# Three changes of instruction order in a fused sequence-mix and BitNet feed-forward kernel: statistics tiles moved into the rounding loop, weight preparation redistributed over the pairs, and the stages of the output projection re-sequenced

## What is computed

```python
# state-space mix with 256 complex states, then LayerNorm
Bu_re, Bu_im = x @ gB_re.T, x @ gB_im.T
h[t] = A * h[t-1] + Bu[t]                      # complex
y = H_re @ C_re.T - H_im @ C_im.T + D * x
x1 = layernorm(x + y)
# feed-forward with 8-bit activations and ternary weights
h = x1 * rsqrt(mean(x1**2) + eps) * norm_w
q(a) = clip(round(a * s), -127, 127) / s       # s = 127 / max|a| of the token
w(W) = clip(round(W / m), -1, 1) * m           # m = mean|W| of the whole matrix
value, gate = split(q(h) @ w(w_gv).T)          # 16384 outputs
h2 = value * silu(gate)                        # 8192 wide
out = layernorm(x1 + (x1 + q(h2) @ w(w_out).T))
```

## Time and profile before

| | |
|---|---|
| time, median of 3 runs (lowest, highest) | 6579.42 us (6553.91, 6587.52) |
| the profiled execution: its own time | 6587.52 us |
| its span on the slowest core (core 1) | 6585.9 us |
| spans of the 8 cores | 6539.1 to 6585.9 us |
| mean granted TensorE clock | 0.776 to 0.780 on all cores |
| TensorE matmul busy | 3338.1 us (51%) |
| VectorE (DVE) | 2360.6 us (36%) |
| ScalarE (ACT) | 1403.7 us (21%) |
| GpSimd (POOL) | 859.6 us (13%) |

### The profile page before, as it was taken

One profiled execution on the slowest core, in us unless ns is written; L12 is line 12 of the kernel. 1 busy time (PEld: TensorE's weight loads), 2 busy tenths in 40 slices (PEclk: granted clock), 3 DMA queues, 4 the chain that ended last, 5 costly groups with the idle time before them and its releaser, 6 DMA issues.

```text
span 6585.9 us, 44872 instructions; the slowest of 8 cores (6539.1 to 6585.9 us)
## 1 busy us (share of the span) xinstructions
PE 3338.1 (51%) x13489; PEld 1315.9 (20%) x13489; DVE 2360.6 (36%) x3177; ACT 1403.7 (21%) x1134; POOL 859.6 (13%) x933
## 2 busy tenths in 40 slices
PE   1223303319998897566556880604560455055545
PEld 0100000004333333222222330201120122012211
DVE  1323464562332232222222336174227422732242
ACT  2222122124444443344444320000000000000000
POOL 0110010011111111111111111010201020102002
PEclk9756656659999998788878995857785788578877
DMA  8234364365555553444544511303430343034334
GB/s 223 91 114 124 100 204 132 91 175 155 145 151 138 143 150 105 134 147 139 151 144 138 135 44 35 102 29 94 136 99 29 96 140 95 29 98 140 92 90 128
DMA packets 682744, 774.87 MB, mean 118 GB/s; under 512 B 24412, under 2 KB 585727, under 8 KB 649223
## 3 DMA queue, kind: packets, MB, share of 16 engines
q1 hardware_dynamic: 617768, 444.78, 25.3%
q10 hardware_dynamic: 27648, 201.34, 9.5%
q0 software_dynamic: 37088, 125.87, 5.7%
HBM read 662.83 MB, written 117.44 MB: 118 GB/s over the span
## 4 chain that ended last, share of the span: by engine, by line
DMA 25%; PE 24%; DVE 22%; issue 12%; ACT 8%; POOL 7%; DVEq 1%; SPq 0%; ACTq 0%; POOLq 0%
PE psA L971 7%; DMA WR<-wq2sp 6%; PE psA L776 5%; DMA P<-wgvT 4%; PE psB L776 3%; ACT HBF L728 3%; POOL CBF L796 3%; DMA x1sp<-OTS 3%; DMA WR<-wgvT 2%; DMA WOF<-woutT 2%; PE psB L971 2%; DMA WOF<-wgvT 2%; DMA WR<-woutT 2%; DMA wq2sp<-P 2%; DVE HBF L788 2%
## 5 line engine op out<-in xcount | busy, mean ns | idle before, releaser
L971 PE MATMUL psA<-P,WR 128*128 128x512 bf16 x3072 | 700.7, 385 | 899.2 <-DMA WR<-wq2sp 892.2
L776 PE MATMUL psA<-P,MNA 128*128 128x512 bf16 x2048 | 498.4, 403 | 276.4 <-DVE CBF L801 266.9
L776 PE MATMUL psA<-P,CBF 128*128 128x512 bf16 x2048 | 492.7, 399 | 261.3 <-DVE CBF L801 245.7
L971 PEld LDWEIGHTS psA<-P,WR 128*128 128x128 bf16 x3072 | 294.9, 99 | 1320.6 <-issue 1002.9
L776 PE MATMUL psB<-P,CBF 128*128 128x512 bf16 x2048 | 457.4, 379 | 9.6
L776 PE MATMUL psB<-P,MNA 128*128 128x512 bf16 x2048 | 457.4, 379 | 9.6
L796 POOL TENSOR_TENSOR CBF<-HBF,P 128x1024 f32<-128x1024 f32 x128 | 299.2, 2337 | 1222.1 <-ACT HBF L793 1186.2
L1028 ACT ACTIVATE P<-Z2S 128x512 f32<-128x512 f32 x64 | 40.3, 629 | 1654.2 <-DVE Z2S L1008 1654.2
L776 PEld LDWEIGHTS psA<-P,MNA 128*128 128x128 bf16 x2048 | 205.5, 102 | 568.4 <-issue 368.4
L776 PEld LDWEIGHTS psA<-P,CBF 128*128 128x128 bf16 x2048 | 204.4, 102 | 548.7 <-issue 345.4
L793 ACT ACTIVATE HBF<-HBF 128x1024 f32<-128x1024 f32 x128 | 135.2, 1057 | 716.7 <-DVE HBF L788 716.7
(11 more groups left out here) (213 smaller groups left out, 3951.8 us busy)
## 6 DMA issues: line engine op xcount, KB each, us to landing
P<-wgvT SPq DMA_DIRECT2D x128, 1024.0 KB
WR<-wq2sp SPq DMA_DIRECT2D x256, 512.0 KB
WOF<-wgvT ACTq DMA_DIRECT2D x64, 1024.0 KB, 5.8
WR<-wgvT ACTq DMA_DIRECT2D x64, 1024.0 KB, 5.8
WOF<-woutT SPq DMA_DIRECT2D x64, 1024.0 KB
h2sp<-CBF POOLq DMA_DIRECT2D x128, 256.0 KB, 4.6
WOF<-woutT ACTq DMA_DIRECT2D x32, 1024.0 KB, 6.5
WR<-woutT ACTq DMA_DIRECT2D x32, 1024.0 KB, 5.8
```

What stands on the lines that cost most here:

```text
L776: sv=sv, last=last: t.matmul(PS[:, (vg * 2 + tq) * 512:(vg * 2 + tq + 1) * 512], WQap(sv + vg)[:, a * 128:(a + 1) * 128], P1[:, a * T + th ...
L971: seg=seg, PSm=PSm: t.matmul(PSm(ds), WR[:, sl * 2048 + jj * 256 + ds * 128: sl * 2048 + jj * 256 + (ds + 1) * 128], P1[:, seg * 16384 + j ...
```

## The change

Three edits.

1. The mix of a tile becomes a function `emit_mix_a(q, a)`. The 16 tiles of quarter 0 are written ahead of the loop. Tile a of quarter q+1 is written inside the round loop of quarter q, behind the rounding of tile a. Rows, normalize, token maxima and the 20 chunks of |w_gv| stay where they were.
2. In the pairs, four chunks of |w_out| are written per pair for p < 16 (two for p < 32 before); the scale of w_out follows at p = 16 (p = 32); then two preparations per pair (three).
3. In the output projection, segment 0 of the next quarter is multiplied before the rows and the output of the present one.

```diff
     emit_xload(0)
+    for a in range(DT):
+        emit_mix_a(0, a)
     for q in range(NQ):
-        for a in range(DT):
...
         b.op("vector", lambda v: v.tensor_scalar(
             repr_(0), psB[0:1, 1024:1536], 1.0 / D, None, OP.mult),
...
             round_neg(k, P1[:, a * T + q * 512:a * T + (q + 1) * 512],
                       R("P1", a * T + q * 512, a * T + (q + 1) * 512, es=2))
+            if q + 1 < NQ:
+                emit_mix_a(q + 1, a)
         for ci in range(50 + q * 20, min(NGV, 70 + q * 20)):
             emit_abs_chunk(wgv_chunk(ci), ci)
...
-        if p < 32:
-            emit_abs_chunk(wout_chunk(2 * p), NGV + 2 * p)
-            emit_abs_chunk(wout_chunk(2 * p + 1), NGV + 2 * p + 1)
-        elif p == 32:
+        if p < 16:
+            for ii in range(4):
+                emit_abs_chunk(wout_chunk(4 * p + ii), NGV + 4 * p + ii)
+        elif p == 16:
...
         elif woj[0] < PAIRS:
-            n = 3 if p < 60 else 8
-            for _ in range(n):
+            for _ in range(2):
...
     d_rowsQ(0)
     d_quant(0, 0)
+    d_mm(0, 0)
+    d_quant(0, 1)
     for q in range(NQ):
-        d_mm(q, 0)
-        d_quant(q, 1)
         if q + 1 < NQ:
             d_rowsQ(q + 1)
             d_quant(q + 1, 0)
         d_mm(q, 1)
+        if q + 1 < NQ:
+            d_quant(q + 1, 1)
+            d_mm(q + 1, 0)
         d_rowsL(q)
         d_apply(q)
```

More of the change, by code:

```diff
@@ L527, in emit_xload @@
                 writes=R("P2", lo * 512, (lo + 4) * 512))
+    def emit_mix_a(q, a):
+        bank = a % 2
+        for im in range(2):
+            for nh in range(2):
+                CT = CBF if nh == 0 else CBF2
+                cn = "CBF" if nh == 0 else "CBF2"
+                HT = HBF if im == 0 else HBF2
+                hn = "HBF" if im == 0 else "HBF2"
+                b.op("tensor", lambda t, q=q, a=a, im=im, nh=nh, bank=bank,
+                     CT=CT, HT=HT: t.matmul(
+                    PSA(bank), CT[:, im * D + a * 128:im * D + (a + 1) * 128],
+                    HT[:, nh * T + q * 512:nh * T + (q + 1) * 512],
+                    start=(im == 0 and nh == 0), stop=(im == 1 and nh == 1)),
+                    reads=R(cn, im * D + a * 128, im * D + (a + 1) * 128, es=2) +
+                          R(hn, nh * T + q * 512, nh * T + (q + 1) * 512, es=2),
+                    writes=[RA(bank)], inc=(im == 1 and nh == 1))
+        b.op("vector", lambda v, a=a, bank=bank: v.scalar_tensor_tensor(
+            P2[:, a * 512:(a + 1) * 512], P2[:, a * 512:(a + 1) * 512],
+            colD[:, a:a + 1], PSA(bank), OP.mult, OP.add),
+            reads=R("P2", a * 512, (a + 1) * 512) + [("colD", 0), RA(bank)],
+            writes=R("P2", a * 512, (a + 1) * 512))
+        b.op("tensor", lambda t, a=a: t.matmul(
+            psB[0:1, 1024:1536], c_onesc[:], P2[:, a * 512:(a + 1) * 512],
+            start=(a == 0), stop=(a == DT - 1)),
+            reads=R("P2", a * 512, (a + 1) * 512) + [("c_onesc", 0)],
+            writes=[RB(2)] if a in (0, DT - 1) else [], inc=True)
+        sq = a % 2
+        b.op("scalar", lambda s, a=a, sq=sq: s.activation(
+            Z2S[:, sq * 512:(sq + 1) * 512], P2[:, a * 512:(a + 1) * 512],
+            AF.Square),
+            reads=R("P2", a * 512, (a + 1) * 512),
+            writes=R("Z2S", sq * 512, (sq + 1) * 512))
+        b.op("tensor", lambda t, a=a, sq=sq: t.matmul(
+            psB[0:1, 1536:2048], c_onesc[:], Z2S[:, sq * 512:(sq + 1) * 512],
+            start=(a == 0), stop=(a == DT - 1)),
+            reads=R("Z2S", sq * 512, (sq + 1) * 512) + [("c_onesc", 0)],
+            writes=[RB(3)] if a in (0, DT - 1) else [], inc=True)
@@ L1083, in build_program @@
     d_quant(0, 0)
-    for q in range(NQ):
-        d_mm(q, 0)
-        d_quant(q, 1)
-        if debug and q == 0:
-            b.dma("sync", lambda s: s.dma_start(out=tapA2[:], in_=P1[:]),
-                  reads=R("P1", 0, DT * T, es=2), q="Dout")
+    d_mm(0, 0)
+    d_quant(0, 1)
+    if debug:
+        b.dma("sync", lambda s: s.dma_start(out=tapA2[:], in_=P1[:]),
+              reads=R("P1", 0, DT * T, es=2), q="Dout")
+    for q in range(NQ):
         if q + 1 < NQ:
```

## The result

| | before | after |
|---|---|---|
| median of 12 runs (lowest, highest) | 6598.03 us (6553.91, 6646.1) | 6714.51 us (6654.45, 6837.54) |
| profiled execution's own time | 6587.52 us | 6686.74 us |
| its span, slowest core (core 1 in both) | 6585.9 us | 6684.2 us |
| pairs, last store of h2 of pair 0 to that of pair 63 | 2429.5 us | 2439.2 us |

After takes 1.0135 times as long as before (95% interval 1.0093 to 1.0177): slower by 1.35%, where 6655 to 6579.4, or 1.0115, was forecast.

The account below looks back on a forecast made before the run. No engine is busy much over half the span, so the order of work binds, stage by stage. Edits 1, 2 and 3 at +110, -20 and -14 sum to +76 us: median 6655 us, +1.2%, own range 6620 to 6700.

Parts of the forecast that it names:

- normalize: Quarter cycle, DVE's normalize stage: 69.1 us falls to 53, as the chunk loads no longer run beside it.
- token maxima: Quarter cycle, DVE's token maxima stage: 22.3 us falls to 19.8, with less beside its small transfer.
- round with mix: Quarter cycle, merged round loop: 5.6 us per tile, 90 us for sixteen, between full clock (83) and half clock (109).
- last square to `Sqrt`: Quarter cycle, 20 chunks on ACT ahead of `Sqrt`, 4.94 us apart: 100.7 us, against 4.1 before.
- such a feedback: Merged loop: a slow loop keeps TensorE busier, which brings the full clock back; hence 5.6 us per tile.
- rival 2: Merged loop: TensorE keeps the full clock through 2 us pauses, 83.2 us for 90, three times; 6635 us, chance 0.15.
- entry term: Pairs, start of the preparations: about 10 us extra for the first pairs, whose weights are no longer ahead.
- +6 and +3: Output projection: ends of `d_apply` (+6 us, under weight loads) and of `d_mm(q+1,0)` (+3, under rounding) no longer hidden.
- term of -8: Output projection: weight loads follow rounding directly, 8 us before DVE is done, saving 8 us.
- Rivals 3 and 4: Pairs with two preparations cost less: rival 3, 35.2 us each, 6517 us, chance 0.08; rival 4, 37.5, 6591, 0.11.
- Rival 1: Merged loop: TensorE stays at 1.2 GHz, 109 us for 90, three times, +57; 6712 us, chance 0.13.
- Rival 5: Pairs: weights come too late and hold up the signs, 44 us per pair, +144; 6799 us, chance 0.05.

Follow-up runs that it names:

- edit 1 alone: Only the mix moved into the round loop, against the kernel before: 6720.47 us, ratio 1.0145 (1.0117 to 1.0173).
- edit 1 with the chunks moved: Kernel before plus merged mix, 12 chunks per quarter (0 to 2) ahead of normalize and 8 inside the merged loop: 6475.78 us, ratio 0.9767.
- edit 2 alone: Only the pairs' new spread of chunks and preparations, against the kernel before: 6647.96 us, ratio 0.9975 (0.9945 to 1.0004).
- two preparations alone: Kernel before with two preparations per pair from p = 33, two chunks per pair kept for p < 32: 6522.6 us, ratio 0.9861.

## Why the prediction was right, and where its terms were off

The direction, the mechanism and its place held: edit 1 makes the kernel slower, by a wait of DVE for a `Sqrt` behind 20 chunks. The runs show this from both sides, edit 1 alone and edit 1 with the chunks moved. That the sum came out near is in part luck: on core 1 edit 1 cost 20 us less than forecast and edits 2 and 3 came out 43 us worse. The terms, each against its measurement in the two profiled executions:

| term | predicted | core 1 | mean of the eight cores |
|---|---|---|---|
| normalize | 53 us | 51.9 | |
| token maxima | 19.8 | 18.3 | |
| round with mix, 16 tiles | 90 (83 to 109) | 84.0 | |
| last square to `Sqrt` | 100.7 | 102.05 | |
| three cycles of a quarter | +110 | +87.8 | +94.0 |
| edit 1, all up to pair 0 | +110 | +90.0 | +96.5 |
| 16 intervals with four chunks | 42.9 each | 42.9 | 42.8 |
| 32 intervals with two preparations, entry included | 1274 | 1306 | 1274 |
| edit 2 | -20 | +10 | -5.5 |
| edit 3 | -14 | -1 | -10.1 |
| sum | +76 | +99 | +81 |

**Edit 1** was mis-sized in the term "round with mix": 84.0 for 90. With 1.5 less in the maxima, 1.1 less in normalize and 1.4 more behind the last square this makes 7.3 per cycle, 22 us in three. The squares are 5.07 and 5.5 us apart in turn. TensorE's timeline, in which two sums take 1.02 us and four matmuls 1.04 at 2.4 GHz:

```profile
953.23 1.02 PE L550 MATMUL psB<-P,c_onesc 128*1 128x512 f32 x2 [2.23 <-DVE P L545]
...
958.29 1.02 PE L550 MATMUL psB<-P,c_onesc 128*1 128x512 f32 x2 [2.22 <-DVE P L545]
959.15 1.55 PE L561 MATMUL psB<-Z2S,c_onesc 128*1 128x512 f32 x2
960.64 1.89 PE L538 MATMUL psA<-HBF,CBF 128*128 128x512 bf16 x4
963.54 1.02 PE L550 MATMUL psB<-P,c_onesc 128*1 128x512 f32 x2 [1.01 <-DVE P L545]
...
1010.67 1.86 PE L550 MATMUL psB<-P,c_onesc 128*1 128x512 f32 x2 [2.23 <-DVE P L545]
...
1014.17 1.04 PE L538 MATMUL psA<-HBF,CBF 128*128 128x512 bf16 x4
```

Between 958 and 1014 us the clock falls to 1.2 GHz in every second tile, six times, in a burst that follows a pause of 2.2 us, and is at 2.4 GHz in the burst after the next pause, of 1.01 us. The pause alone does not decide it: the burst at 953.23 followed one of 2.23 us and kept the full clock. The slow stretch also wanders forward, from the end of its burst (960.64) to the beginning (1010.67), where the four matmuls of the same burst are fast again (1014.17). The prediction had such a feedback (a slow loop keeps the engine busier, and that brings the clock back); the rows agree with it, but no run tests it. It priced the slow stretches too high. They lie mostly beside DVE's own 5.07 us and add 0.2 to 0.5 us to every second tile. So the time came out where rival 2 put it (83.2), but not for its reason, that the clock would not fall. The rule of the Trainium skill that stood beside that rival ("TensorE: Matmul & The Clock Gate", section "Why this matters for your kernels") has the engine keep its clock through pauses as short as these; the granted clock of 0.83 in this stretch and the rows above say otherwise.

**Edit 2** missed on core 1 by its entry term. The four-chunk intervals were 42.9, the one with the scale 40.4 (41.4), the last 14 took 406 us (405), and of the 32 with two preparations the last 25 averaged 39.3 (39.5; the terms given for it, 39.3 and 1.5 less 0.8, make 40.0). But the first seven took 323.7 us where 276.5 was forecast, with 10 more for the entry. ACT's timeline after, a second preparation in one of these pairs and one of later:

```profile
2436.61 2.00 ACT L744 ACTIVATE P<-WOF,colS 128x2048 bf16<-128x2048 f32 x1 [17.63 <-DMA wq2sp<-P]
...
3052.13 2.00 ACT L744 ACTIVATE P<-WOF,colS 128x2048 bf16<-128x2048 f32 x1 [11.86 <-DMA wq2sp<-P]
```

The wait for the store of the one before is some 6 us longer at first: on core 1 a store landed 10.9 us after its issue there (median), in the later pairs 7.3. The core's own DMA engines did not carry more (busy 51% at 125 GB/s in the first seven intervals, 54% at 150 GB/s in later ones), and it is not so on every core: the first seven took 320 and 324 us on cores 0 and 1, 301 and 291 on 2 and 3, and 270 to 275 on 4 to 7. With edit 2 alone it was cores 4 and 5 that took longest (320 us, the others 287 to 305), and with two preparations alone cores 6 and 7 (318 and 315 us, the others 277 to 289). What delays the stores there was not tested; the cause stays open.

In the mean of the cores the entry cost what was forecast (290.4 us for 286.5), and the pairs took 2406.0 us, where the sum of the prediction was 2406. The forecast of -20 counted from the 2429.5 us of core 1, 18 above the mean of the cores before. And in four other kernels, whose pairs are those of before, the slowest core took 2443.1 to 2475.5 us for them, so 10 us more or less on one core is no measure of edit 2. The runs of edit 2 alone say 0.9945 to 1.0004, -37 to +3 us: the sign of edit 2 by itself is not settled.

**Edit 3** missed on core 1 by one term. SP's timeline after, one cycle:

```profile
4932.45 130.73 SPq L965 DMA_DIRECT2D WR<-wq2sp  x32
5063.28 56.65 SPq L1067 DMA_DIRECT2D Z2S<-z2sp  x16
5119.99 147.50 SPq L938 DMA_DIRECT2D CBF<-h2sp  x32
5267.60 14.62 SPq L965 DMA_DIRECT2D WR<-wq2sp  x4
...
5443.67 142.48 SPq L938 DMA_DIRECT2D CBF<-h2sp  x32
5586.25 133.64 SPq L965 DMA_DIRECT2D WR<-wq2sp  x32
```

The corresponding rows of before that the earlier trace rows do not hold:

```profile
4696.35 56.02 SPq L1063 DMA_DIRECT2D Z2S<-z2sp  x16
...
4885.66 284.10 SPq L934 DMA_DIRECT2D CBF<-h2sp  x64
5169.86 13.89 SPq L961 DMA_DIRECT2D WR<-wq2sp  x4
...
5351.59 54.42 SPq L1063 DMA_DIRECT2D Z2S<-z2sp  x16
```

The cycle is 653.8 us (4932.45 to 5586.25), 1.4 less. `d_mm(q,1)` holds SP for 176.1 (181.7 before), -5.6, where -5.3 was forecast for the rows. `d_mm` of segment 0 went from 133.2 to 130.8, -2.4 for a forecast of -3.1. The two stretches of `d_quant` went from 284.2 to 290.2 together, +6.0, as against +6 and +3 forecast, and `d_apply` added 0.6. The term of -8, weight loads that follow rounding directly, does not exist: before, too, they follow it at once (5169.86, where the loads of `d_quant` end). In the mean of the cores edit 3 came nearer to its forecast: from one L1063 (L1067 after) to the next the first cycle went from 654.5 to 650.1 us and the second from 657.4 to 649.4, and all behind the pairs took 10.1 us less, where -14 was forecast.

**The rivals.** Rivals 3 and 4, cheap preparations, fell: the settled pairs with two preparations took 39.3 us. Rival 1 fell by the loop at 84. Rival 5's 44 us per pair did occur on core 1, in seven pairs of 32, but behind a store and not behind the weights.

## What to carry to other kernels

When work is moved into an earlier loop, list what it is moved past in every engine's own stream: a batch of transfers that was hidden there becomes a wall for the short instruction behind it. Spread filler work in portions that each stage can hide, and look for the price of the next portion, not the mean. Before reordering stages, see whether one queue strings them together; here the choice of the queue was worth 5.4% and the order of the stages nothing that the runs could tell. And when the terms of a small difference are read from traces, read them on every core: on the slowest core alone two of the three edits here looked worse than in the mean of the eight.

## What the hardware showed that was not expected

- TensorE's clock alternated in the merged loop with a period of two tiles, with pauses of 2.2 and 1.0 us in turn, and the loop lost only 0.2 to 0.5 us in two tiles by it.
- The first seven intervals with two preparations took up to 20% longer on two neighbouring cores than on others of the same execution (320 and 324 us for 270 to 275), and in other kernels it was another two cores.
- Moving 128 KB loads from SP's queue to POOL's saved 88 us per cycle, though the same bytes move on the same engines; each issue took 0.54 us of POOL, and the load landed after 2.7 us. The Trainium skill ("DMA: Bandwidth & Descriptors", section "Issuing engines are not separate DMA queues") lets several issuers save only the time on the sequencer that it takes to start the DMAs. This case shows a larger effect beside it: a load no longer stands behind others that wait for their buffers.
